# A graph layer on one core: stage 1 from a static table, with six even batches on GpSimd and one read of x per batch

## What is computed

```python
h = jnp.maximum(_layernorm(x, axis=-1), 0.0)       # x is (64, 128, 1024): batch, t, node
xp = jnp.transpose(h, (2, 0, 1))                   # node, batch, t
x_avg = xp.mean(axis=1)                            # mean over the 64 batches
x_norm = x_avg / jnp.maximum(jnp.linalg.norm(x_avg, axis=-1, keepdims=True), 1e-12)
sim = (x_norm @ x_norm.T + 1.0) * 0.5
adj = (sim + gumbel0 > 1.0 - sim + gumbel1)        # then a graph Wn from adj and common neighbours
xw = jnp.einsum('nbt,to->nbo', xp, weight)
out = x + transpose(jnp.einsum('sd,sbt->dbt', Wn, xw) + bias)
```

## Time and profile before

| | us |
|---|---|
| median of 3 runs | 954.95 (954.63 to 955.58) |
| the profiled execution | 955.32 |
| its span, first to last instruction | 953.6 |

### The profile page before, as it was taken

The page is one execution under the profiler, slowest core; times in us unless marked ns, Lnnn a source line. Parts: engine busy times, 40 slices in busy tenths (PEclk is TensorE's granted clock), DMA queues, the critical chain, the costliest instruction groups (busy, mean ns, idle before and its releaser), DMA issues.

```text
span 953.6 us, 12576 instructions
## 1 busy us (share of the span) xinstructions
PE 908.6 (95%) x4615; PEld 771.2 (81%) x4619; DVE 725.9 (76%) x1499; ACT 352.3 (37%) x565; POOL 213.6 (22%) x178
## 2 busy tenths in 40 slices
PE   2988899888999999999999999999999999999997
PEld 0655565777888888888898888888988888888886
DVE  7789678899978879785767675858676766767587
ACT  3999817431212121223333334242424242424130
POOL 2677733002211111120111111111111111111111
PEclk9999999999999999999999999999999999999999
DMA  9999981301707244342433424152424242424022
GB/s 357 351 350 343 393 328 61 134 23 44 252 30 249 81 184 147 118 168 98 135 131 110 156 92 175 66 192 74 177 89 177 89 176 89 177 68 175 29 105 89
DMA packets 36587, 149.75 MB, mean 157 GB/s; under 512 B 2864, under 2 KB 2992, under 8 KB 33456
## 3 DMA queue, kind: packets, MB, share of 16 engines
q1 hardware_dynamic: 36528, 148.97, 42.8%
HBM read 107.02 MB, written 41.94 MB: 156 GB/s over the span
## 4 chain that ended last, share of the span: by engine, by line
PE 83%; DVE 8%; ACT 4%; issue 2%; DMA 1%; SPq 0%; ACTq 0%; DVEq 0%
PE ps L1346 67%; PE ps L1286 7%; ACT main L496 3%; DVE bmem L945 3%; PE ps L1120 2%; PE ps L1141 2%; PE ps L1208 2%; PE ps L1189 1%; DVE bmem L938 1%; DVE stats L732 1%; DMA main<-in_x 1%; ACT bmem L522 0%; DVE main L1056 0%; DVE bmem L957 0%; PE ps L1265 0%
## 5 line engine op out<-in xcount | busy, mean ns | idle before, releaser
L1346 PE MATMUL ps<-bmem,main 128*128 128x256 f32 x3136 | 692.5, 380 | 3.0 <-DVE main L1023 2.6
L1346 PEld LDWEIGHTS ps<-bmem,main 128*128 128x128 f32 x3136 | 590.7, 190 | 80.8 <-DVE main L1023 3.0
L466 POOL TENSOR_TENSOR main<-main 128x256 f32<-128x256 f32 x32 | 25.2, 788 | 541.6 <-ACT main L633 482.8
L1023 DVE TENSOR_TENSOR main<-ps,main 128x512 f32<-128x512 f32 x124 | 76.4, 622 | 83.9 <-PE ps L1346 83.9
L604 ACT ACTIVATE main<-ps 128x512 f32<-128x512 f32 x88 | 52.5, 597 | 210.9 <-PE ps L1286 210.9
L1032 DVE TENSOR_TENSOR main<-main 128x256 f32<-128x256 f32 (+1 forms) x256 | 119.3, 536 | 0.0
L456 POOL TENSOR_TENSOR main<-main 128x256 f32<-128x256 f32 (+1 forms) x96 | 92.0, 986 | 119.1 <-DVE main L1016 119.1
L1286 PEld LDWEIGHTS ps<-w_sb,main 128*128 128x128 f32 x704 | 92.4, 192 | 9.0 <-issue 2.8
L1286 PE MATMUL ps<-w_sb,main 128*128 128x128 f32 x704 | 93.5, 276 | 3.9 <-ACT main L604 3.9
L1141 PE MATMUL ps<-main,ident 128*128 128x512 f32 x128 | 63.2, 628 | 26.6 <-ACT main L496 26.6
L863 DVE TENSOR_TENSOR main<-main 128x256 f32<-128x256 f32 x112 | 46.9, 419 | 54.5 <-PE ps L1346 51.2
(11 more groups left out here) (98 smaller groups left out, 534.5 us busy)
## 6 DMA issues: line engine op xcount, KB each, us to landing
main<-in_x SPq DMA_DIRECT2D x61, 1024.0 KB, 6.7
out<-main SPq DMA_DIRECT2D x31, 1024.0 KB, 4.9
main<-in_x SPq DMA_DIRECT2D x50, 512.0 KB, 5.7
bmem<-in_L_gnn_gumbel SPq DMA_DIRECT2D x8, 1024.0 KB, 8.0
spill<-bmem SPq DMA_DIRECT2D x8, 1024.0 KB, 14.5
main<-spill SPq DMA_DIRECT2D x8, 1024.0 KB, 6.9
out<-main SPq DMA_DIRECT2D x1, 512.0 KB, 4.9
out<-main SPq DMA_DIRECT2D x2, 256.0 KB, 4.6
```

The costliest lines, as they stand in the source:

```text
L1023: dve.tensor_tensor(at, piece(slot, b), at, ALU.add).then_inc(s, 1)
L1346: last = pe.matmul(piece(slot, b)[:, QUARTER * e:QUARTER * (e + 1)], left_[:, blk(c)], right_[:, c, :], start=slot in FRESH and b < 3 and ...
```

## The change

It has five parts.

- The hardware loops of stage 1 are gone; all engines run through a table, `GROUPS`: [0], [1, 2], [3, 4], ..., [29, 30], [31]. So a group's pairs are (odd, even) where they were (even, odd). VectorE finishes the first three groups whole before it starts the next (`t < 3`), then puts the steps between the statistics as before, and ends with a group of one pair.
- `POOLED` = 6, 10, 14, 18, 22, 26: for the even batch of these pairs GpSimd itself computes max(x * rstd, mean * rstd) in place in `xin` (`tensor_scalar`), and adds it. That is relu(x * rstd - mean * rstd) + mean * rstd; VectorE notes mean * rstd in `floor` for each, sums the six columns, and subtracts the sum when it adds PSUM to `hsum`.
- Each batch of x has a load and a semaphore of its own, 0.5 MB each, issued when its own half of the slot is free; that of a pooled batch waits for GpSimd's addition (`s_even`).
- The last pair's even batch is added by TensorE too, not by GpSimd, and both late products of pair 30 stand behind the last pair's sums.
- `SPILLED` becomes 1, 3, 5, 9, 13, ..., 25, each copied to `kept` three pairs later, always after the second pair of a group; `AHEAD` becomes 0, 2. The number of products is unchanged.

The diff, cut to its core:

```diff
+    SPILLED = [1, 3, *range(5, PAIRS - 3, 4)]
+    AHEAD = [0, 2]
+    GROUPS = [[0], *([p, p + 1] for p in range(1, PAIRS - 1, 2)), [PAIRS - 1]]
+    GROUP_OF = {p: t for t, pairs in enumerate(GROUPS) for p in pairs}
+    POOLED = [p for p in range(4, PAIRS - 2) if p % 4 == 2]
...
+                for b in range(2):
+                    before = p - XPAIRS
+                    if before >= 0 and before in POOLED and b == 0:
+                        sp.wait_ge(s_even, before + 1)
+                    elif before >= 0:
+                        sp.wait_ge(s_h, 2 * before + 1 + b)
+                    sp.dma_start(xin[:, p % XPAIRS, b, :], x[2 * p + b, :, :]
+                                 ).then_inc((s_x if b else s_x_first)[p % XPAIRS], 16)
...
+            for p in range(PAIRS - 1):
+                if p in POOLED:
+                    n = 2 * p
+                    at = xin[:, p % XPAIRS, 0, :]
+                    pool.wait_ge(s_row, GROUP_OF[p] + 1)
+                    j = POOLED.index(p)
+                    pool.tensor_scalar(at, at, rstd[:, n:n + 1], floor[:, j:j + 1], ALU.mult, ALU.max
+                                       ).then_inc(s_norm, 1)
+                    pool.wait_ge(s_norm, j + 1)
+                    wait(pool, s_even, p)
+                    pool.tensor_tensor(hsum[:, :], hsum[:, :], at, ALU.add).then_inc(s_even, 1)
...
+            std(0)
+            for t, pairs in enumerate(GROUPS):
+                for p in pairs:
+                    if t == 0 or t == len(GROUPS) - 1:
+                        relu(p)
+                        if t == 0:
+                            std(1)
+                    elif p == pairs[0] and t > 1:
+                        relu(p)
+                        std(t + 1)
...
+                    if p - HPAIRS + 1 in SPILLED:
+                        keep(p - HPAIRS + 1)
...
+                for p in GROUPS[t]:
+                    if p in POOLED:
+                        j, b = POOLED.index(p), 2 * (p - GROUPS[t][0])
+                        dve.scalar_tensor_tensor(out=floor[:, j:j + 1], in0=mean[:, b:b + 1], scalar=1.0,
+                                                 in1=again[:, b:b + 1], op0=ALU.mult, op1=ALU.mult).then_inc(s_floor, 1)
...
+                if t < 3:
+                    for c in range(steps):
+                        last = long_step(t, c)
+                    last.then_inc(s_bn, 1)
+                    aggregate(t)
+                    whole_chain(t)
...
+                else:
+                    long_step(t, 0)
+                    long_step(t, 1)
+                    for c, between in enumerate((aggregate, invert, quotient, newton, set_rstd, set_shift), 1):
+                        if t > 3:
+                            between(t - 1)
+                        last = long_step(t, c + 1)
...
-                dve.tensor_tensor(hsum[:, half(f)], ps[:, f, :], hsum[:, half(f)], ALU.add).then_inc(s_sum, 1)
+                dve.scalar_tensor_tensor(out=hsum[:, half(f)], in0=ps[:, f, :], scalar=dmax[:, 0:1],
+                                         in1=hsum[:, half(f)], op0=ALU.subtract, op1=ALU.add).then_inc(s_sum, 1)
...
+            for p in range(PAIRS):
+                pe.wait_ge(s_h, 2 * p + 2)
+                for b in ((0, 1) if p == PAIRS - 1 else (1,)):
...
+            pe.wait_ge(s_kept, KEPT)
+            late_times_weight(0, 2)
```

More of the change, by code:

```diff
@@ L675, in aggregate, with batches, invert @@
+            def batches(t):
+                return slice(2 * GROUPS[t][0], 2 * GROUPS[t][-1] + 2)
+            def aggregate(t):
+                dve.wait_ge(s_bn, t + 1)
+                for b in range(2 * len(GROUPS[t])):
+                    last = dve.bn_aggr(mv[:, t % 2, b, :], stats[:, t % 2, b, :])
                 last.then_inc(s_mv, 1)
-            def invert(g, turn, b0=0, b1=4):
-                half, _, _, inv, *_ = rows(g, b0, b1)
-                dve.wait_ge(s_std, turn + 1)
+            def invert(t):
+                half, _, _, inv, *_ = rows(t)
+                dve.wait_ge(s_std, t + 1)
@@ L1126, in late_times_weight, with keep_product @@
                 times_weight(h1[:, pair % HPAIRS, n % 2, :], first_bank).then_inc(s_late_hw, 1)
[L1128 to L1139 removed]
+            def keep_product(p, b):
+                n = 2 * SPILLED.index(p) + b
+                wait(pe, s_kept, n - 1)
+                times_weight(h1[:, p % HPAIRS, b, :], 2 + 2 * b).then_inc(s_hw, 1)
```

276 lines of the change are left out of this document (87 added, 189 removed).

## The result

The changed kernel took **960.69 us** (median of 4 runs, 960.57 to 961.02), the kernel before, run beside it, 954.79 us (4 runs, 954.32 to 955.58). The ratio is **1.0063**, 95% interval 1.0047 to 1.0079: slower by 5.9 us. The forecast was 954.8 with a range to 957.7, so it was wrong, and the range too. The profiled span went from 953.6 to 959.3 us, +5.7.

A forecast was written before the change was run, and what follows sets the result against it. Stage 1 was taken as bound by ScalarE and VectorE waiting for each other, not loads. Relus ending 2.5 us sooner, less 2.3 given back at TensorE's handover, made -0.2 us: 954.8 us, range 952.6 to 957.7.

The forecast's parts named there:

- X: Stage 1, GpSimd: time of one scaling of a pooled batch, taken as 1.5 us between rows of 0.95 and 2.39.
- it begins to cost at X near 3.2: Stage 1, GpSimd: slots of h1 and four additions to catch up at the end hide scalings up to near 3.2 us.
- Rival C: Stage 1: GpSimd is the bound if a scaling takes over 3.2 us; at 4, +4 us, 959; chance 0.06.
- A slot now waits for GpSimd's addition: 0: Stage 1, five places: x slots held until GpSimd's addition cost 0; for pair 10, 9 us are enough.
- Five of six pooled relus worth 0: Stage 1, ScalarE: five removed relus lie in periods without copies, already idle for shift; periods stay 5.50 us, gain 0.
- The sixth, put at 0.9: Stage 1, pair 6: its period also has copies, so removing its relu cuts 6.53 to 5.6 us, gaining about 0.9.
- 0.6 us for one product that TensorE has late: Middle of stage 1: 0.6 us added to 60.2 us for ten periods, as copies wait for one late TensorE product.
- Rival D: Start of stage 1: TensorE's clock rises only at 32 us, copies of pairs 1 and 3 late, 957.5; chance 0.06.
- The start: Start of stage 1: pair 0 alone, first relu at 8.3 us, then whole groups with roots at 13.8, 20.4 and 28.1.
- The tail: End of stage 1, TensorE: four halves and two products follow the last relu; column sums at 119.5, 2.3 us given back.
- Part 2, one load per batch: 0: Stage 1 loads: 0.5 MB singles supply a batch per 1.45 us against 1.50 needed, so cost 0.
- rival B: Stage 1: 0.5 MB loads set the pace, slower than a batch per 1.50 us; +2.7 us, 957.7 at 1.60; chance 0.13.

The follow-up runs named there:

- experiment 4: Changed kernel with the six pooled scalings in six different GpSimd instruction forms, five not normalising correctly, to time each form; run once, 957.16 us.
- experiment 5: Changed kernel with six more GpSimd instruction forms in the six pooled places, none the reference's normalisation, to time each; run once, 960.33 us.
- experiment 1: Changed kernel with POOLED empty: no scaling, floor or subtraction, while table, single loads and tail stay as changed; 956.78 us, ratio 1.0019.
- experiment 3: Changed kernel with three pooled batches (pairs 6, 14, 22) in place of six; 957.26 us, ratio 1.0022.
- experiment 7: Changed kernel, all six pooled, GpSimd writing the scaled batch into h1 so the x slot is freed at the scaling's end; 960.09 us, ratio 1.0052.
- experiment 6: Changed kernel with three pooled batches (pairs 12, 16, 20) in groups whose period also holds ScalarE's two copies; 958.38 us, ratio 1.0039.
- experiment 11: experiment 10 plus two pooled batches (pairs 12 and 20) in periods with copies, written to h1 as in experiment 7; 951.13 us, ratio 0.9964.
- Experiment 2: experiment 1 with pair 30's first late product moved ahead of the last pair's sums on TensorE; 956.48 us, ratio 1.0013.
- Experiment 9: experiment 1 with the copy of pair 1's products moved before the square root of group (5,6); 955.02 us, ratio 1.0000.
- experiment 10: Experiment 2 and Experiment 9 together, with GpSimd instead of TensorE adding the last pair's even batch; 952.54 us, ratio 0.9975.
- experiment 12: experiment 1 with x loaded as before the change: first three pairs by batch, then 1 MB per pair; 956.85 us, ratio 1.0029.

## Why the prediction was wrong

**The step that failed is the price of the scaling.** The prediction said that no row showed X, and bounded it by the nearest rows, the memset of 0.95 us and the two-input addition of 2.39, and took 1.5. It measured 3.78. The upper bound was no bound: it rested on the number of tensors read, while what decides is the operation (experiments 4 and 5), and no row of the trace before has a maximum on GpSimd. The prediction's limit, "it begins to cost at X near 3.2", was not what failed. A round is 13.7 us, of which the four additions with their gaps take 9.9 (the prediction had 9.6 without gaps), so GpSimd falls behind from X = 12.03 - 9.9 = 2.1 us on. The end hides some of that. An estimate: without the scaling's delay the column sums would start near 121.6 (121.02 of experiment 1 and the later first load), which leaves the last addition until 119.5, 3.7 us before 123.20; spread over the five scalings behind GpSimd's last wait, the queue begins to cost at X near 3.0. No run has such an X.

**Rival C was the mechanism**, at a chance of 0.06. It had the right places (the slot late, GpSimd's last addition late) and 959 us at X = 4. It came to 960.7 at 3.78, with the last addition at 123.20 in place of 120.7. Experiments 1, 3, 4 and 7 bear it out: without pooled batches 3.9 us of the 5.9 are gone, three batches cost about 0.5, six cheaper ones in the same places nothing, and freeing the slot sooner moves the relus 1.5 us but the column sums only 1.1, since VectorE then waits 7.16 us for GpSimd.

**"A slot now waits for GpSimd's addition: 0"** fell with the same step. For pair 10 the 9 us of cushion were counted on a GpSimd that is idle between additions. With one that falls behind 1.7 us a round the cushion was used up, and VectorE waited for x 1.21 us at 88.23 and 2.08 at 102.44. The price of a wait was read from the first one in the series, not from the last.

**Five of six pooled relus worth 0: right.** Where GpSimd keeps up ScalarE idles up to 1.8 us for `shift` in the period of a pooled batch, and it still lasts 5.50 (experiment 3). Experiments 6 and 11 show the other side: the same batch in a period with copies shortens it from 6.53 to 5.5. The sixth, put at 0.9, was worth nothing in the end: its period (35.18 to 42.58) lasted 7.4 us because a copy waited 1.89 us for its product.

**The middle: "0.6 us for one product that TensorE has late": mis-sized.** In the table without pooled batches the period from 34.57 is 7.32 in place of 6.53 and the next 7.01 in place of 6.53, 1.3 us together; in the changed kernel it was 7.40 and 7.01. The prediction took a product at 1.78 us; after a gap of 3.22 and 3.35 us in TensorE's queue one took 3.62 and 3.47. Experiment 2 has the same code there as experiment 1 and a product of 2.05 us, no copy waited, and its relus end 1.3 us sooner: that is the price of the slow product. Experiment 9 moved the copy that caused the gap, and the column sums start 1.6 us sooner than in experiment 1 (medians 1.8, or 1.5 against the kernel before beside each). Rival D had this mechanism near (a clock that comes late, copies late behind it), but placed it in the first rise.

**The start was right to 0.8 us**: first relu 9.07 (forecast 8.3), of which 0.7 are the first load (landed at 4.83, before at 4.12); in experiment 1 the roots agree within 0.2 us. **The tail was right**: two products between the last pair and the column sums, 2.3 us given back there; experiment 10 gets 2.3 back by undoing it.

**Part 2, one load per batch: 0, right** (experiments 1 and 12: 956.78 and 956.85). No run supports rival B. The Trainium skill (DMA: Bandwidth & Descriptors, Bandwidth) asks for transfers of 1 MiB or more; with several of 0.5 MB under way in one queue the two sizes gave the same time. That does not refute the rule, since both kernels wait for slots and not for loads; but early in the stage, slices of 2.9 us reached 423 GB/s with the small loads (experiment 1) and 425 with the large (experiment 12), so the smaller size was no handicap here. The other page that the prediction weighed (the Trainium skill, GPSIMD Engine Reference, Instruction dispatch) has about 6 us for the first call to a freshly loaded kernel. No such gap is in the trace: the first scaling starts at 36.57, when the addition of 34.23 has ended, and takes 3.79 us, as the fifth does.

The sum then, column sums against before: -0.2 forecast; +0.7 for the product's size and +0.9 for the sixth batch make +1.4, as experiment 1 has it (+1.35); the late first load adds 0.6 and GpSimd 3.8, which makes the +5.7 measured.

## What to carry to other kernels

An operation that the trace does not show has no upper bound from rows of other operations: where a change hinges on it, work out the price at which the engine falls behind (here 2.1 us, with every gap in the round counted) and the one at which that reaches the end (near 3.0 by the estimate above), and give the case beyond it a chance that fits how little is known. Work taken off an engine gains only in the periods in which that engine is the bound (two batches in the right periods gave 2.1 us of the column sums and 1.4 of the median, five in the wrong ones nothing), and only as long as the engine that receives it can finish a round within a round. A queue that is over its rate by 1.7 us in 12 shows no cost at first and its whole cost at the end; follow it to its last instruction, and follow every buffer that its work sets free.

## What was not expected of the hardware

GpSimd's `tensor_scalar` over 128 x 1024 f32 takes 1.11 to 1.19 us for a multiplication with a multiplication or an addition, and 3.63 to 3.79 us as soon as one of the two is a maximum, with pointers or constants; one multiplication alone, or one maximum alone, takes 2.85. The Trainium skill (GPSIMD Engine Reference, Engine selection) calls work with one input roughly line-rate on GpSimd, beside about twice slower for two inputs. By the rows, that holds for the copy (1.04) and the fused forms without a maximum, while the form used here is 1.6 times the two-input addition (3.78 against 2.36).

TensorE's clock fell in the middle of stage 1. Windows of the changed kernel (columns as in the earlier trace rows):

```profile
29.00:33.00 4.00, 0.84 (x5) 0.84 (x6) 4.00 (x14) 4.00 (x5) 2.35 (x1) 0.94 1.03 410
33.00:37.00 4.00, 4.00 (x17) 3.16 (x16) 3.16 (x13) 4.00 (x6) 2.77 (x2) 0.63 1.03 410
```

TensorE was busy 0.84 us of the four from 29 us, and the granted clock averaged 0.63 in the next four: mostly the lower of its two levels, 1.2 GHz, after the upper one of 2.4. The product in it took 3.47 us instead of 1.95, and in ScalarE's next period a copy waited 1.89 us for the product behind it. In the kernel before, and in experiment 9 (idle for 2.33 us there), the clock was at 1.00 from 29 to 37 us. In experiment 2 it was as well, although TensorE was idle for 2.1 us there, and that execution was 1.3 us ahead. The profiles of all kernels with the new table agree. In the nine in which TensorE stood idle for 3.1 to 5.1 us before that product, it took 3.19 to 3.79 us. In the others (idle for 2.1 us in experiment 2, and for 2.33 and 0.66 us in experiments 9 and 10 and 0.67 in 11, before a row of sums) no product there took over 2.05 us. The length of the idle time depends in turn on how fast TensorE worked just before: the product near 21 us took 3.13 us in experiment 2, and the idle time was 2.1; in experiment 3 the products before took 1.95, and it was 5.0. Whether the fall comes in every execution of one kernel was not measured: each has one profile.
